# A graph layer with linear attention and a mixture of experts: GpSimd's turn awaited at its own border, two accumulators for the path sums, five banks for the early shared units, target numbers loaded first

## The reference, cut to what matters

```python
xn = layernorm(x)                                   # x: 625 nodes x 512
# graph part: 10625 edges, 64 paths (i1, i2, i3), 16 segments of 32 columns
contrib  = coef[None, :, None] * xn[src][:, i1, :] * edge_attr[:, i2, :]
edge_out = zeros.at[:, i3, :].add(contrib);  gnn = zeros.at[dst].add(edge_out)
# linear attention over all 625 rows, 8 heads of 64, 32 random features
q, k = elu(q @ R) + 1, elu(k @ R) + 1
z = q @ (k.T @ v) / (q @ k.sum(0) + 1e-6);  mix = z @ W_out + b_out
x = x + gnn + mix
# mixture of experts on xr = layernorm(x): 2 shared experts, 64 experts, top 6
prob = softmax(xr @ Wr);  top 6 kept, divided by their sum = gate
x = x + xr + sum_shared swiglu(xr) + sum_e gate[:, e] * swiglu_e(xr)
```

## Time and profile before

| what | value |
|---|---|
| median of 3 runs | 1051.81 us (1047.87 to 1056.03) |
| the profiled execution: its time, its span | 1057.01 us, 1055.2 us |
| TensorE busy | 930.3 us (88%) |
| VectorE busy | 545.7 us (52%) |
| GpSimd busy | 297.1 us (28%) |
| ScalarE busy | 242.4 us (23%) |
| products, L1146 | 640 instructions, 235.3 us |
| path sums, L1226 | 128 instructions |
| GpSimd's copy of one element, L667 | 8 instructions, 37.3 us |

### The profile page before, as it was taken

One profiled execution on the slowest core, in us unless ns is written; L12 is line 12 of the kernel. 1 busy time (PEld: TensorE's weight loads), 2 busy tenths in 40 slices (PEclk: granted clock), 3 DMA queues, 4 the chain that ended last, 5 costly groups with the idle time before them and its releaser, 6 DMA issues. The chain is left out here.

```text
span 1055.2 us, 20491 instructions
## 1 busy us (share of the span) xinstructions
PE 930.3 (88%) x7283; PEld 616.6 (58%) x7283; DVE 545.7 (52%) x1676; ACT 242.4 (23%) x567; POOL 297.1 (28%) x258
## 2 busy tenths in 40 slices
PE   2699999968885678999999999999999999999970
PEld 2365566645542676666666666667666776666640
DVE  6899999958879863323223333333223333332206
ACT  2111111102221201223223222232232332222220
POOL 4336463854001012222222222222222232222110
PEclk9899999989998788999999999999999999999995
DMA  9656575474458804788977999999887999998548
GB/s 304 239 200 234 211 240 200 133 267 147 113 155 343 325 10 141 287 326 329 400 257 297 410 411 410 392 338 405 326 305 282 394 415 381 360 408 336 186 157 340
DMA packets 77186, 301.08 MB, mean 285 GB/s; under 512 B 13803, under 2 KB 14192, under 8 KB 58693
## 3 DMA queue, kind: packets, MB, share of 16 engines
q1 hardware_dynamic: 57208, 254.36, 63.7%
q0 software_dynamic: 17280, 38.48, 10.3%
q10 hardware_dynamic: 2572, 6.58, 1.8%
HBM read 290.40 MB, written 27.14 MB: 301 GB/s over the span
## 5 line engine op out<-in xcount | busy, mean ns | idle before, releaser
L1731 PE MATMUL bank<-arena,low 128*64 128x256 f32 x2784 | 320.0, 383 | 0.0
L1731 PEld LDWEIGHTS bank<-arena,low 128*64 128x64 f32 x2784 | 195.7, 137 | 101.9 <-issue 11.9
L1146 DVE TENSOR_TENSOR arena<-arena 128x288 f32 (+1 forms) x640 | 235.3, 442 | 27.9 <-DMA arena<-xn_d,ssel 11.6
L1590 PE MATMUL bank<-arena,multi 128*64 128x256 f32 x1408 | 168.4, 395 | 33.3 <-DVE arena L1146 33.2
L1360 DVE TENSOR_TENSOR low<-low,bank 128x256 f32<-128x256 f32 x87 | 53.4, 614 | 259.0 <-ACT low L928 259.0
L1740 PE MATMUL bank<-arena,low 128*64 128x256 f32 x1392 | 161.2, 379 | 1.1 <-ACT low L925 1.1
L1590 PEld LDWEIGHTS bank<-arena,multi 128*64 128x64 f32 x1408 | 103.5, 142 | 95.3 <-issue 37.8
L708 POOL DMA_INDIRECT low<-xr_d,idx x64 | 90.3, 1410 | 235.2 <-DVE place L1355 163.1
L712 POOL DMA_INDIRECT y_d<-low,place x64 | 65.7, 1027 | 297.6 <-ACT low L932 208.0
L1740 PEld LDWEIGHTS bank<-arena,low 128*64 128x64 f32 x1392 | 100.1, 137 | 51.2 <-ACT low L925 1.3
L932 ACT ACTIVATE low<-bank,gcol 64x256 f32<-64x256 f32 x174 | 81.8, 470 | 105.6 <-PE bank L1740 104.5
(11 more groups left out here) (196 smaller groups left out, 644.3 us busy)
## 6 DMA issues: line engine op xcount, KB each, us to landing
arena<-in_L_ffn_Wg_dram SPq DMA_DIRECT2D x64, 1024.0 KB, 9.5
arena<-in_L_ffn_Wu_dram SPq DMA_DIRECT2D x64, 1024.0 KB, 11.8
arena<-in_L_ffn_Wd_dram SPq DMA_DIRECT2D x64, 1024.0 KB, 8.9
arena<-in_edge_attr_dram SPq DMA_DIRECT2D x88, 256.0 KB
arena<-y_d SPq DMA_DIRECT2D x6, 1250.0 KB, 12.0
sums_d<-arena ACTq DMA_DIRECT2D x18, 256.0 KB, 6.9
arena<-sums_d SPq DMA_DIRECT2D x4, 896.0 KB
arena<-in_L_mix_W_qkv_dram SPq DMA_DIRECT2D x2, 1024.0 KB, 11.3
```

What stands on the lines that cost most here:

```text
L1146: return dve.tensor_tensor(prod[:, buf, 0:n, EXT * p:EXT * p + EXT], x1[b][:, 0:n, bass.ds(i1, EXT)], x2[b][:, 0:n, bass.ds(i2, EXT)], ALU ...
L1590: ins = pe.matmul(bank[2 * b + c // 2][64 * h:64 * h + 64, 256 * (c % 2):256 * (c % 2) + 256], pair[:, pairs, i, :], prod[:, buf, i, 256 * ...
L1731: ins = pe.matmul(out_bank[64 * h:64 * h + 64, w * HF:(w + 1) * HF], xgT[:, b, k, 64 * o:64 * o + 64], gu[:, slot, w, k, h * HF:(h + 1) * HF],
```

## The change

It has these parts. (1) VectorE awaits at the border of window w (1 to 8) the turn that GpSimd takes after window w-1, for its gather of window w+1. For that the choice of the last windows' edges (`turn_ends(2)`, `take_ends(2)`, `count_hits`) moves one chunk ahead, from k = 2, 4, 6 to k = 1, 3, 5, on VectorE and TensorE. (2) `normalize` sits behind the sixth product of its chunk and not behind the twelfth. (3) A path sum is one instruction over all five tiles; even paths add into `x_sb`, odd ones into a second accumulator `acc`. `acc` is set by a DMA on SP's queue that broadcasts `b_out` to 125 rows of 5 x 512; it is issued when the last `mix_values` is done, since it lies where `kp` and `qp` were, and the matmul with the row of ones is gone. Five adds join `acc` to `x_sb`. (4) The early shared units use five banks (3 to 7) in turn and are put further ahead on TensorE; the three strided copies into `rtab` go to ScalarE, from three buffers `parts`; the wait for the flags comes behind the first expert's gate and up on TensorE, and behind its first register load on ScalarE. (5) ScalarE's queue loads the target numbers before the first window's ends.

```diff
@@ -126,9 +126,9 @@
     m["rm2"] = low[:, 8180:8244]
-    m["bout"] = low[0:1, 8244:8756]
     m["wv"] = m["wout"] = low[:, 8756:10804].rearrange("p (c n) -> p c n", c=DC)
+    m["acc"] = low[0:TR, 0:2560].rearrange("p (t d) -> p t d", t=TT)
     m["xr"] = low[0:TR, 0:2560].rearrange("p (t d) -> p t d", t=TT)
@@ -147,7 +147,8 @@
     m["selb"] = multi[:, 320:480].bitcast(BF16).rearrange("p (t e) -> p t e", t=TT)
-    m["part_b"] = multi[:, 480:640].bitcast(BF16).rearrange("p (t e) -> p t e", t=TT)
+    m["parts"] = [t.bitcast(BF16).rearrange("p (t e) -> p t e", t=TT)
+                  for t in (multi[:, 480:640], low[:, 7232:7392], low[:, 7392:7552])]
     m["cnt_row"] = multi[0:1, 640:896]
...
@@ -453,7 +453,7 @@
-            return bank[3 + u % 2] if u < WINDOW else bank[7]
+            return bank[3 + u % 5] if u < WINDOW else bank[7]
@@ -495,7 +495,6 @@
                     sp.dma_start(rm2[HD:128, FD:2 * FD], rm).then_inc(s_rm, 16)
-                    sp.dma_start(bout_row, bout.rearrange("(o d) -> o d", o=1)).then_inc(s_rm, 16)
                 if w == 3:
@@ -517,6 +516,9 @@
             for h in range(2):
+                if h == 1:
+                    sp.wait_ge(s_zp, 2 * TT)
+                    sp.dma_start(acc, bout.rearrange("(o t d) -> o t d", o=1, t=1).to_broadcast([TR, TT, D])).then_inc(s_rm, 16)
                 sp.wait_ge(s_last[h], 32)
@@ -567,7 +569,7 @@
                 load_down(e, wd[e])
-            sp.wait_ge(s_path_sum, 2 * PATHS)
+            sp.wait_ge(s_path_sum, PATHS)
             for e in range(2, GU_RING):
@@ -642,7 +644,6 @@
             pool.iota(steps[:, :], pattern=[[CAP2, 4]], base=CAP2, channel_multiplier=0, allow_small_or_imprecise_dtypes=True)
-            pool.memset(one_row[:, :], 1.0)
             pool.memset(one_col[:, :], 1.0)
@@ -745,8 +746,8 @@
         def _(act):
+            load_edges(act, dst_i, dst)
             load_first_ends(act, 1, dst)
-            load_edges(act, dst_i, dst)
@@ -900,7 +901,7 @@
                 act.copy(xT[:, :, t * TR:(t + 1) * TR], bank[4 + t % 2][:, 0:DC * TR].rearrange("p (c n) -> p c n", c=DC)).then_inc(s_xrT, 1)
-            act.wait_ge(s_lmax, 1)
+            act.wait_ge(s_gates, 1)
             act.activation(prob[0:TR, :, :], prob[0:TR, :, :], ACT.Exp).then_inc(s_exp, 1)
@@ -913,6 +914,9 @@
             for u in range(WINDOW):
+                if 2 <= u < 5:
+                    act.wait_ge(s_gates, u)
+                    act.copy(rtab[:, :, :, 2 + u].rearrange("p e t -> p t e"), parts[u - 2][0:TR]).then_inc(s_rtab, 1)
                 shared_silu(u)
@@ -936,12 +940,9 @@
             act.wait_ge(s_base, 1)
-            act.wait_ge(s_flags, 1)
             act.wait_ge(s_xgTp, 1)
...
             for e in range(NX + 1):
-                if e % PLACES == 0 and e < NX:
-                    act.load(over[e % 16:e % 16 + PLACES], vrow[:, e:e + PLACES])
                 if e + 1 < NX:
@@ -960,6 +961,10 @@
                     scale(0, bank[5], (e - 1) % PLACES, (e - 1) % 2).then_inc(s_ys, 1)
+                if e % PLACES == 0 and e < NX:
+                    if e == 0:
+                        act.wait_ge(s_flags, 1)
+                    act.load(over[e % 16:e % 16 + PLACES], vrow[:, e:e + PLACES])
                 if e < NX:
@@ -1160,8 +1165,8 @@
                 if c == 0:
-                    if w >= 2:
-                        dve.wait_ge(s_turn, w - 1)
+                    if 1 <= w < NW - 1:
+                        dve.wait_ge(s_turn, w)
                     dve.wait_ge(s_x2[b], landed(w))
@@ -1175,16 +1180,16 @@
                         one_hots(b, w * G, PER[w])
-                    if k == 2 and p == 4:
+                    if k == 1 and p == 4:
                         turn_ends(2)
-                    if k == 4 and p == 4:
+                    if k == 3 and p == 4:
                         dve.wait_ge(s_chosen, 4)
...
                         count_hits()
-                    if k == 6 and p == 4:
+                    if k == 5 and p == 4:
                         dve.wait_ge(s_chosen, 5)
                         dve.tensor_scalar(more_v[:, :], bank[3][0:1, 300:301], float(E), None, ALU.is_lt).then_inc(s_cover, 1)
-                    if k in (32, 33, 36, 37) and p == 12:
+                    if k in (32, 33, 36, 37) and p == 6:
                         normalize((32, 33, 36, 37).index(k))
@@ -1218,13 +1223,12 @@
             def path_sum(path, reg):
-                at = dve.snap(reg, min_val=0, max_val=D - EXT)
-                for half, (lo, hi) in enumerate(((0, 3), (3, TT))):
-                    if path > 0:
-                        dve.wait_ge(s_path_sum, 2 * path + half - 1)
-                    seg = x_sb[:, lo:hi, bass.ds(at, EXT)]
-                    dve.scalar_tensor_tensor(seg, sums[:, lo:hi, column(path):column(path) + EXT], coef[0:TR, path:path + 1], seg,
-                                             ALU.mult, ALU.add).then_inc(s_path_sum, 1)
+                to = x_sb if path % 2 == 0 else acc
+                if path > 1:
+                    dve.wait_ge(s_path_sum, path - 1)
+                seg = to[:, :, bass.ds(dve.snap(reg, min_val=0, max_val=D - EXT), EXT)]
+                dve.scalar_tensor_tensor(seg, sums[:, :, column(path):column(path) + EXT], coef[0:TR, path:path + 1], seg,
+                                         ALU.mult, ALU.add).then_inc(s_path_sum, 1)
@@ -1232,6 +1236,7 @@
             dve.wait_ge(s_sums[1], 32)
+            dve.wait_ge(s_rm, 48)
             for path in range(32):
@@ -1241,7 +1246,10 @@
-            dve.wait_ge(s_path_sum, 2 * PATHS)
+            dve.wait_ge(s_path_sum, PATHS)
+            for t in range(TT):
+                ins = dve.tensor_tensor(x_sb[:, t, :], x_sb[:, t, :], acc[:, t, :], ALU.add)
+            then(dve, ins)
             for t in range(TT):
@@ -1290,7 +1298,7 @@
             then(dve, dve.tensor_reduce(r1[:, 0], L5, AX, ALU.max))
-            dve.tensor_tensor(P5, L5, wide(r1[:, 0]), ALU.subtract).then_inc(s_lmax, 1)
+            dve.tensor_tensor(P5, L5, wide(r1[:, 0]), ALU.subtract).then_inc(s_gates, 1)
             dve.wait_ge(s_exp, 1)
@@ -1320,15 +1328,14 @@
             dve.wait_ge(s_place, 1)
-            dve.tensor_tensor(rtab[:, :, :, 3].rearrange("p e t -> p t e"), E5, wide(sixes[0:TR, :]), ALU.add)
-
+            dve.tensor_tensor(rtab[:, :, :, 3].rearrange("p e t -> p t e"), E5, wide(sixes[0:TR, :]), ALU.add).then_inc(s_rtab, 1)
+
+            shared_mult(1)
             for k in range(3):
-                tcol = rtab[:, :, :, 4 + k].rearrange("p e t -> p t e")
-                then(dve, dve.tensor_copy(part_b[0:TR], G5))
-                dve.tensor_copy(tcol, part_b[0:TR])
-                then(dve, dve.tensor_tensor(G5, G5, part_b[0:TR], ALU.subtract))
-            dve.sem_inc(s_rtab, 1)
-            shared_mult(1)
+                dve.tensor_copy(parts[k][0:TR], G5).then_inc(s_gates, 1)
+                dve.wait_ge(s_gates, k + 2)
+                if k < 2:
+                    then(dve, dve.tensor_tensor(G5, G5, parts[k][0:TR], ALU.subtract))
@@ -1360,19 +1367,17 @@
-            shared_mult(2)
             dve.wait_ge(s_place, 1)
-            dve.wait_ge(s_rtab, 1)
             hot(0, rank[:, 0], 0).then_inc(s_hot, 1)
             hot(1, rank[:, 1], 0).then_inc(s_hot, 1)
+            shared_mult(2)
             shared_mult(3)
             for e in range(LEAD):
+                shared_mult(4 + e)
                 dve.wait_ge(s_look, e + 1)
...
                 hot(e % 2, rank[:, e + 2], 0).then_inc(s_hot, 1)
-                if e < 2:
-                    shared_mult(4 + 2 * e)
-                    shared_mult(5 + 2 * e)
+            shared_mult(7)
@@ -1512,7 +1517,7 @@
                 if t == 0:
-                    pe.wait_ge(s_rm, 48)
+                    pe.wait_ge(s_rm, 32)
                 if t >= 2:
@@ -1578,10 +1583,9 @@
                     pe.wait_ge(s_flush, NW - 1)
-                pe.matmul(at, one_row[:, 0:TR], bout_row, start=True, stop=False)
                 for k in range(DC):
                     ins = pe.matmul(at, zT[:, t, k, :], wout_sb[:, k, :],
-                                    start=False, stop=(k == DC - 1))
+                                    start=(k == 0), stop=(k == DC - 1))
                 ins.then_inc(s_op, 1)
@@ -1615,10 +1619,10 @@
                     project_k(k + 2)
-                if k == 2:
+                if k == 1:
                     pe.wait_ge(s_choose, 4)
                     turn_ends(2, bank[3])
-                if k == 4:
+                if k == 3:
                     pe.wait_ge(s_choose, 5)
@@ -1687,8 +1691,8 @@
                     pe.wait_ge(s_shh, u)
-                elif u >= 2:
-                    pe.wait_ge(s_shh, u - 1)
+                elif u >= 5:
+                    pe.wait_ge(s_shh, u - 4)
                 if u == UPS:
@@ -1743,6 +1747,7 @@
             shared_up(1)
+            shared_up(2)
             pe.wait_ge(s_selb, 1)
@@ -1751,25 +1756,21 @@
```

(16 more changed lines are left out.)

5 lines of the change are left out of this document (2 added, 3 removed).

## The result

The kernel after takes 1043.79 us (median of 16 runs, 1042.29 to 1047.42), the kernel before, run beside it, 1053.98 (16 runs, 1044.74 to 1057.24). The ratio is 0.993, 95% interval 0.9906 to 0.9954. I had forecast 1021 us, a ratio of 0.971. The runs of before scatter: six take 1044.7 to 1048.9 us, nine 1052.8 to 1057.3 and one 1051.8; its profiled execution (1057.01 us) is among the longest. The profiled execution of after took 1044.62 us, with a span of 1042.5, so 12.7 us of span were won where 30.9 were forecast.

The account below looks back on a forecast made before the run. TensorE paces windows 0 to 6 and the experts, VectorE leads from 231 to 305 us. 10.3 + 4.7 + 3.9 + 12.0 = 30.9 us off 1057.01 gives 1026.1; 5.2 lower for the median, forecast 1021, range 1011 to 1034.

Parts of the forecast that it names:

- Part 1: Turns in the windows: GpSimd's copy gets through at the border, window 7's wait for gathers goes; 10.3 us won.
- rival (c): Window 7 was made late by DMA traffic, not GpSimd's copy, so the 11.2 us stay: 1032 us; chance 0.05.
- 11.2 less 0.9: Windows: wait of 11.64 us goes and 0.48 comes, 11.2 won; 0.5 lost at window 8, 0.4 at window 1.
- Part 2: Reciprocals: issue stalls behind four `normalize` shrink to 0.5 and 1.1 us each; 4.7 us won, bounds 0 to 7.9.
- Part 3: Path sums and adds: 32.0 us becomes 21.8, less a 6.3 us wait for `acc` (load 11.5 us); 3.9 us won.
- Rival (a): Load of `acc`: only five of sixteen DMA engines work on 125 rows, 13.3 us and 2 to land: 1025; chance 0.2.
- (b): Path sums: each takes its whole duration before the next, 0.376 x 64, 6.8 us more: 1028; chance 0.1.
- (d): Path sums: `acc` lands early and the pitch is 0.23, 5.2 + 2.6 us won: 1013; chance 0.07.
- Rival (e): Load of `acc`: all 625 pieces read one row of DRAM, 62.8 us, slower than before: 1072; chance 0.04.
- Part 4: Routing: TensorE's holes filled or shortened and two slow shared units at full speed; 12.0 us won, bounds 7.7 to 14.
- rival (f): Routing: TensorE only trades the flags for other waits, 10 us less won: 1031; chance 0.04.
- Part 5: Start: target numbers come earlier but the chain stops again at 24.75 us; 0, bounds 0.5 won to 1.5 lost.

Follow-up runs that it names:

- e4: Kernel before with part 1 alone (turns at their own borders, choices one chunk ahead), but `more_v` left in chunk 6: 1058.81 us, ratio 0.9938.
- third group: Runs beside the kernel before (1049.18 us): the best version 1021.11 us; that version without part 4 1035.82, without part 2 1023.60, without part 1 1021.17.
- the fifth: Group beside the kernel before (1064.93 us): the best version with 36 unread matmuls ahead of the transposes, 1040.24 us; the same without part 1, 1040.27.
- the best version: Kernel after with `more_v` in chunk 6, `acc` zeroed by GpSimd with the bias by matmul, and the first ends loaded first: 1021.11 us, ratio 0.9722.
- c0_after: The kernel after again, with one register operation more in each of some 23 overflow branches: 1045.36 us, ratio 0.9948.
- a1_cover_k6: Kernel after with only the write of `more_v` moved back from chunk 5 to chunk 6: 1037.31 us, ratio 0.9851.
- a3_acc_two_loads: Kernel after with the load of `acc` cut into two, of 112 and 13 partitions: 1040.84 us, ratio 0.9893.
- b1_small_op_k5: Kernel after with `more_v` in chunk 6 and an unread one-element multiply on VectorE in chunk 5: 1058.16 us, ratio 0.9932.

## Why the prediction was wrong

**Part 1 (10.3 us forecast) is the step that failed.** The mechanism was right: the copy gets through at the border, the wait at window 7 goes, a border costs 0.5. The failed sentence is "GpSimd and its queue are behind no new wait, since the copy only gets shorter". I had costed the choices pulled ahead at 0.4 us on VectorE and TensorE, and had not asked what GpSimd does in that chunk: it issues the gathers of window 2. So the new wait stood in the sum at nothing and measured 10.20 us. The stall that I removed at 187 us came back at 72 us in the same shape, a GpSimd instruction that gets through only at a break of VectorE's products; that copy and gather are held by one and the same thing isn't shown. The rows of the copy were the warning, and I applied them to the copy alone. My rival (c), traffic, is refuted by the kernel after and by e4, where the wait at window 7 goes.

The turns themselves were also mis-sized: 6.3 us by the medians of e4 and 4.0 in the profiles of the third group, not 11.2 less 0.9. I took the wait from a single execution. It follows the length of the copy, and that varies: 18.35 us and 11.64 of wait in before, 12.45 and 2.73 without part 1 in the third group, 18.36 and 11.76 at another border in the fifth, and copies of 6.55 us made no wait. The forecast also began from 1057.01 us, one of the longest times of before, and carried the gain over to the median whole.

**Part 2 (4.7)** held in the gaps and won less in the time. Behind the four `normalize` the gaps are 1.67, 0.80, 0.24 and 0.76 us, 3.5 together where I had said 3.2: 4.4 us less than before. So the gaps came out as forecast; that register loads make them was argued from the rows and isn't shown. But in the kernel after the last `normalize` waits 1.75 us for TensorE, so part of it is spent there. Undone against the best version it is worth 3.2 us at the first path sum and 2.5 in the median.

**Part 3 (3.9)** is a loss of 2.7. The load took 14.1 us and not 11.5, from 304.64 and not 289.5; the path sums 20.7 and not 18.6; the adds 3.1 as said. The term that was mis-sized is the load, and with the stalled windows in front of it `acc` could not be there at 301.0. Rival (a) had the mechanism, a third of the engines, and came nearer with 13.3 us and 2 to land, 15.3. Rivals (b) and (d) are refuted by the pitch: 0.30 us, neither 0.376 nor 0.23. The Trainium skill, "DMA: Bandwidth & Descriptors", section "Why a DMA increments its semaphore by 16 and not by 1", gives 125 rows five of the 16 engines, 0.31; the trace agrees, with 0.33. The share of 0.37 had stood in the earlier trace rows, and I set the price by bytes per second of other rows all the same. Rival (e), the single row of DRAM, is refuted.

**Part 4 (12.0)** held: 13.4 in the profiles and 14.7 by undoing it, so rival (f) is refuted. TensorE's holes are 2.60 (forecast 1.6) and 1.73 (forecast 2.6).

**Part 5 (0)** cost 1.7 us in the profile, just beyond the bound of 1.5: ScalarE's queue had the ends of the first window later, and VectorE waits for them to 9.41, in the chain that leads to the first gather.

The best version, 1021.11 us, is near my 1021 by luck: it is another kernel, in which the gather of window 2 isn't shut out, nothing is loaded for `acc` and the ends come first.

## What to carry to other kernels

When a small instruction is moved into a run of long VectorE instructions, look at what GpSimd does at that time: an instruction of 0.14 us cost 8 to 10 here. A second accumulator is worth what it saves only if it can be set without a DMA of a count of partitions like 125, which a third of the DMA engines carried; zeros written on an idle engine did it (2.23 us on GpSimd). And a wait that one trace shows may be shorter in the next execution: look at a second trace, and at TensorE's granted clock behind an idle stretch, before booking a gain.

## What I had not expected of the hardware

A gather's issue on GpSimd took 15.98 us in place of 1.1 when it began 1.2 us behind a short VectorE instruction among products without gaps. A compare by either form and a multiply of one element did it in chunk 5; behind the cast of 0.28 us in chunk 1 it took 4.3 to 5.4 us, in all kernels where a gather began behind that cast's start (by 0.1 to 1.2 us). Where the last gather had begun 0.27 us ahead of the cast (c0_after, a1_cover_k6, a3_acc_two_loads, b1_small_op_k5), it took 1.17. Where a pause or another short instruction of VectorE is seen in the trace, the gather ended 0.8 to 0.9 us behind its start. Why the gathers pass while the products are all alike was not found. A load of 125 partitions took 14.1 to 19.2 us for 1.28 MB, at a DMA share of 0.33 where little ran beside it, and 9.8 to 10.8 as 112 and 13.
